# Attention scores from four 32-row slices of TensorE, and the softmax shift moved from GpSimd into ScalarE's exponentials

## The reference

```python
# both layers: 16 heads of depth 16, 77 context rows
logits = einsum('bhqd,bhkd->bhqk', q, k)      # layer 0: q scaled, + bias; layer 1: mask
weights = softmax(logits, axis=-1)            # over the 77 context rows
attn = einsum('bhqk,bhkd->bhqd', weights, v) @ Wo.T
# layer 0 experts: 32, the best four of each row
scores = softmax(flat @ router_w.T + router_bias)
topk_scores, topk_idx = top_k(scores, 4)
topk_scores = topk_scores / topk_scores.sum()
```

## Time and profile before

| | |
|---|---|
| runs of the kernel | 785.07 us median of 3 (783.95 to 786.47) |
| profiled execution | 784.07 us |
| its span, first to last instruction | 782.2 us |
| TensorE's mean granted clock | 0.981 of full |

### The profile page before, as it was taken

The page is one execution under the profiler, slowest core; times in us unless marked ns, Lnnn a source line. Parts: engine busy times, 40 slices in busy tenths (PEclk is TensorE's granted clock), DMA queues, the critical chain, the costliest instruction groups (busy, mean ns, idle before and its releaser), DMA issues.

```text
span 782.2 us, 15464 instructions
## 1 busy us (share of the span) xinstructions
PE 729.4 (93%) x4576; PEld 592.1 (76%) x4577; DVE 457.4 (58%) x1697; ACT 324.7 (42%) x1000; POOL 306.5 (39%) x331
## 2 busy tenths in 40 slices
PE   8799999999998999999999799988997999999994
PEld 4578888856665888888875488777774999999993
DVE  2689999647973544444433779999984232232331
ACT  1345555422221455555543488877850212212210
POOL 1243443300022555555514667763113244344421
PEclk9999999899999999999999999999998999999998
DMA  7423433340014455555872236776521565555530
GB/s 208 150 95 97 141 108 127 109 128 21 14 54 88 140 160 162 163 163 161 135 128 68 68 92 184 218 202 177 154 68 52 188 201 162 194 196 162 196 130 5
DMA packets 64181, 103.05 MB, mean 132 GB/s; under 512 B 20145, under 2 KB 42113, under 8 KB 63860
## 3 DMA queue, kind: packets, MB, share of 16 engines
q1 hardware_dynamic: 52852, 72.88, 29.9%
q0 software_dynamic: 10976, 27.22, 14.1%
q10 hardware_dynamic: 288, 2.10, 0.8%
HBM read 82.83 MB, written 22.07 MB: 134 GB/s over the span
## 4 chain that ended last, share of the span: by engine, by line
PE 64%; DVE 27%; DMA 3%; issue 2%; ACT 2%; POOL 1%; SPq 0%; DVEq 0%; ACTq 0%; POOLq 0%
PE bank L1368 11%; PE bank L1383 10%; PE bank L1316 9%; PE bank L937 5%; DVE U L1626 5%; PE bank L1329 5%; PE bank L1240 4%; DVE mx L1497 3%; DVE X L1488 2%; PE bank L844 2%; PE bank L1307 2%; PE bank L1288 2%; PE bank L923 2%; DMA expert_out<-U 2%; DVE R L1856 2%
## 5 line engine op out<-in xcount | busy, mean ns | idle before, releaser
L622 POOL DMA_INDIRECT U<-normed,idx_all x95 | 90.3, 951 | 141.8 <-PE bank L1307 73.7
L1316 PE MATMUL bank<-R,U 128*128 x380 | 99.2, 384 | 0.1
L1368 PE MATMUL bank<-X,R 128*128 128x128 f32 x736 | 85.9, 275 | 0.0
L1368 PEld LDWEIGHTS bank<-X,R 128*128 128x128 f32 x736 | 84.1, 192 | 0.1
L1383 PE MATMUL bank<-R,X 128*128 (+1 forms) x368 | 83.1, 379 | 0.0
L1977 DVE TENSOR_TENSOR U<-U,bank 128x128 f32<-128x128 f32 x95 | 27.3, 287 | 83.0 <-ACT U L804 82.9
L597 POOL DMA_INDIRECT R<-expert_out,slot x64 | 61.5, 960 | 35.1 <-DMA expert_out<-xr 17.7
L1383 PEld LDWEIGHTS bank<-R,X 128*128 128x128 f32 x368 | 68.2, 190 | 8.4
L691 ACT ACTIVATE U<-U,mx 128x77 f32<-128x77 f32 x256 | 67.3, 352 | 12.6 <-DVE mx L1497 12.6
L1316 PEld LDWEIGHTS bank<-R,U 128*128 128x128 f32 x380 | 65.4, 192 | 5.6 <-issue 0.3
L609 POOL TENSOR_TENSOR U<-U,mx 128x1232 f32<-128x1232 f32 x16 | 36.0, 2249 | 68.9 <-DVE mx L1497 68.9
(11 more groups left out here) (255 smaller groups left out, 1541.2 us busy)
## 6 DMA issues: line engine op xcount, KB each, us to landing
R<-in_w SPq DMA_DIRECT2D x21, 1024.0 KB
R<-in_w SPq DMA_DIRECT2D x40, 256.0 KB
R<-in_gu SPq DMA_DIRECT2D x8, 1024.0 KB, 5.8
expert_out<-U SPq DMA_DIRECT2D x48, 128.0 KB
expert_out<-xr SPq DMA_DIRECT2D x47, 128.0 KB
normed<-xr SPq DMA_DIRECT2D x32, 128.0 KB, 3.1
R<-in_down SPq DMA_DIRECT2D x8, 512.0 KB, 3.6
x<-X SPq DMA_DIRECT2D x16, 128.0 KB
```

The lines of the kernel that those rows point to most:

```text
L622: pool.indirect_dma_start(xg0[i % NXG], None, xn_d[0], bass.IndirectOffsetOnAxis(idx_all[:, i:i + 1], 0)).then_inc(EX[0]["gath"][i % NXG], 16)
L1316: mm = pe.matmul(bank[2 + u][:, 0:2 * F0], xgT0[u][:, c, :], gu_w[:, c, bass.ds(e, 1), :].rearrange("p a n -> p (a n)"), start=(c == 0), s ...
L1368: mm = pe.matmul(bank[1 + 2 * v + f // 4][:, (f % 4) * P:(f % 4 + 1) * P], w1_of[v][:, c, f * P:(f + 1) * P], xgT1[v][:, c, :], start=(c = ...
```

## The change

It does four things.

1. The rows of Wq and Wk (and their biases) are permuted on the host so that bank g's heads lie in rows 32g to 32g+31 of both chunks. `kbd` now holds 2 heads for 32 partitions, 32 rows by 154 columns, and `scores` issues eight matmuls, four row slices of chunk 0 and then four of chunk 1. Both releases of `sc_mm` come in chunk 1, after the sixth and the eighth matmul.
2. In attention 0 GpSimd's subtraction and ScalarE's single exponential go; VectorE negates its maxima there too, and ScalarE takes 16 exponentials per tile, heads 0 to 7 ahead of the third `pT` copy. At t=-1, where there is no `pT` yet, all 16 stand behind `qT`, in attention 1 as well.
3. `dve.max` writes to a tile's own slot of `best0`; the 16 subtractions of the best logit become one of 128x64, at the start of layer 0's experts.
4. In attention 0, `chosen0` of the tile before comes ahead of the cast of the indices.

```diff
+QH, QR = HG // KC, P // NG
-        kbd[0], o = cut(R2, o, (B * KC, HG, S2))
+        kbd[0], o = cut(R2, o, (B * KC, QH, S2))
...
-                    if l == 0 and on(t, 2):
-                        u = par(2)
-                        pool.wait_ge(T["mx"], 2 * n + 6)
-                        s3 = sc[u].rearrange("p (h k) -> p h k", h=H)
-                        pool.tensor_tensor(s3, s3, mx[u][:, :].unsqueeze(2).to_broadcast([P, H, S2]),
-                                           ALU.subtract).then_inc(T["sub"], 1)
...
-                    if l == 1 and on(t, 1):
+                    if on(t, 1) and on(t, 0):
                         ins = exps(t, n, 0)
...
-                    if l == 0 and on(t, 1):
-                        u = par(1)
-                        act.wait_ge(T["sub"], n + 2)
-                        act.activation(sc[u], sc[u], ACT.Exp).then_inc(T["p"], 1)
-                    if l == 1 and on(t, 1):
+                    if on(t, 1) and not on(t, 0):
+                        exps(t, n, 0)
+                    if on(t, 1):
                         exps(t, n, 1).then_inc(T["p"], 1)
...
-                    for g in range(NG):
-                        pe.wait_ge(T["q"], n + 3)
-                        if g % 2 == 0:
-                            need(pe, T["copied"], 2 * n + 3 + g // 2)
-                        c, half = g // 2, g % 2
-                        r = slice(64 * half, 64 * half + 64)
-                        mm = pe.matmul(bank[g][:, 0:HG * S2], qT[r, c, :],
-                                       kbd[l][r, batch(t, 2) * KC + c].rearrange("p h k -> p (h k)"),
-                                       start=True, stop=True)
-                        if half:
-                            mm.then_inc(T["sc_mm"], 1)
+                    pe.wait_ge(T["q"], n + 3)
+                    for c in range(KC):
+                        for g in range(NG):
+                            if c == 0 and g % 2 == 0:
+                                need(pe, T["copied"], 2 * n + 3 + g // 2)
+                            r = slice(QR * g, QR * g + QR)
+                            mm = pe.matmul(bank[g][:, c * QH * S2:(c + 1) * QH * S2], qT[r, c, :],
+                                           kbd[l][r, batch(t, 2) * KC + c].rearrange("p h k -> p (h k)"),
+                                           start=True, stop=True)
+                            if c == KC - 1 and g % 2:
+                                mm.then_inc(T["sc_mm"], 1)
...
-                                      ALU.max, negate=(l == 1)).then_inc(T["mx"], 1)
+                                      ALU.max, negate=True).then_inc(T["mx"], 1)
...
-                        dve.tensor_scalar(wgt[:, bass.ds((t - 2) * TOPK, TOPK)], m8[w][:, 0:TOPK], m8[w][:, 0:1],
-                                          None, ALU.subtract).then_inc(RT["below"], 1)
...
+                    dve.tensor_tensor(wgt[:, :].rearrange("p (t j) -> p t j", t=NT), best0[:, :, 0:TOPK],
+                                      best0[:, :, 0:1].to_broadcast([P, NT, TOPK]), ALU.subtract).then_inc(RT["below"], 1)
```

More of the change, by code:

```diff
@@ L58 @@
 NOH = NT
-TEMP_END = 9276
+TEMP_END = 8660
 VF_BACK = 632
@@ L136, in build @@
             attn_w[1][name], o = cut(U, o, (KC, D))
-        kbd[1], o = cut(U, o, (B * KC, HG, S2))
+        kbd[1], o = cut(U, o, (B * KC, QH, S2))
         vbd[1], o = cut(U, o, (B * PC, 3 * VC))
@@ L223, in build @@
         own_e, tile_less, tok_1 = route1[:, 0:E1], route1[:, E1:E1 + PLAN1], route1[:, E1 + PLAN1:]
-        mask_k = sb("mask_k", [P, HG])
+        mask_k = sb("mask_k", [P, QH])
         mask_v = sb("mask_v", [P, PC, 3])
@@ L247, in build @@
         m8 = [sb(f"m8_{i}", [P, 8]) for i in range(2)]
+        best0 = sb("best0", [P, NT, 8])
         i8 = [sb(f"i8_{i}", [P, 8], U32) for i in range(2)]
@@ L713, in step @@
                         transposed(n, 1)
-                    if l == 1 and on(t, 1):
+                    if on(t, 1) and on(t, 0):
                         ins = exps(t, n, 0)
-                        if t == NT - 2:
+                        if l == 1 and t == NT - 2:
                             ins.then_inc(T["p"], 1)
@@ L805, in _ @@
             experts0_steps(act, experts0)
-            act.wait_ge(RT["below"], NT)
+            act.wait_ge(RT["below"], 1)
             act.activation(wgt[:, :], wgt[:, :], ACT.Exp).then_inc(R0["exp"], 1)
@@ L1433, in keys @@
                         dve.tensor_tensor(kbd[l][:, b * KC + m],
-                                          k_sb[:, b * S2:(b + 1) * S2].unsqueeze(1).to_broadcast([P, HG, S2]),
-                                          mask_k[:, :].unsqueeze(2).to_broadcast([P, HG, S2]),
+                                          k_sb[:, b * S2:(b + 1) * S2].unsqueeze(1).to_broadcast([P, QH, S2]),
+                                          mask_k[:, :].unsqueeze(2).to_broadcast([P, QH, S2]),
                                           ALU.mult).then_inc(K["k_bd"], 1)
@@ L1513, in step @@
                     w, m = par(-2), n - 1
+                    best = best0[:, min(max(t - 2, 0), NT - 1), :] if l == 0 else m8[w][:, :]
                     if l == 0 and isinstance(t, int) and t == -2:
@@ L1542, in step @@
                         wait_apart(dve, RT["lg"], m)
-                        dve.max(m8[w][:, :], lg[:, 0:ne]).then_inc(RT["mx"], 1)
+                        dve.max(best, lg[:, 0:ne]).then_inc(RT["mx"], 1)
                     if l == 1 and on(t, -3):
@@ L1552, in step @@
                         wait_apart(dve, RT["mx"], m)
-                        dve.max_index(i8[w][:, :], m8[w][:, :], lg[:, 0:ne]).then_inc(RT["ix"], 1)
+                        dve.max_index(i8[w][:, :], best, lg[:, 0:ne]).then_inc(RT["ix"], 1)
                     if l == 1 and on(t, 3):
@@ L1562, in step @@
                         row_stats(T, par(3), t + 3)
-                    if l == 0 and on(t, -2):
-                        dve.tensor_scalar(wgt[:, bass.ds((t - 2) * TOPK, TOPK)], m8[w][:, 0:TOPK], m8[w][:, 0:1],
-                                          None, ALU.subtract).then_inc(RT["below"], 1)
                     if on(t, -1):
@@ L1576, in step @@
                                                  op1=ALU.add).then_inc(TL["slot"], 1)
+                    if l == 0 and on(t, -3):
+                        chosen0(t - 3)
                     if on(t, -2):
@@ L1579, in step @@
                         dve.tensor_copy(ef[:, bass.ds((t - 2) * nk, nk)], i8[w][:, 0:nk]).then_inc(RT["ef"], 1)
-                    if l == 0 and on(t, -3):
-                        chosen0(t - 3)
                     if l == 1 and on(t, -2):
@@ L1968, in experts0 @@
                 if isinstance(s, int) and s == 0:
+                    dve.wait_ge(RT["mx"], NT)
+                    dve.tensor_tensor(wgt[:, :].rearrange("p (t j) -> p t j", t=NT), best0[:, :, 0:TOPK],
+                                      best0[:, :, 0:1].to_broadcast([P, NT, TOPK]), ALU.subtract).then_inc(RT["below"], 1)
                     dve.wait_ge(bias_in[1], 16)
@@ L2026, in constants @@
         "ident": np.eye(P, dtype=np.float32),
-        "mask_k": ((p[:, None] % 64) // DH == np.arange(HG)).astype(np.float32),
+        "mask_k": ((p[:, None] % QR) // DH == np.arange(QH)).astype(np.float32),
         "mask_v": ((f // S2)[:, :, None] == (np.array(HEAD0)[None, :, None] + np.arange(3))).astype(np.float32)
@@ L2052 @@
     arrays["ctxT"] = rows_of(a["ctx_1024"].reshape(B * S2, D).T)
+    rows = np.arange(D).reshape(NG, KC, QH * DH).swapaxes(0, 1).reshape(D)
     for l in range(2):
         for w in ("Wq", "Wk", "Wv", "Wo"):
-            arrays[f"L{l}_{w}"] = rows_of(a[f"L{l}_xattn_{w}"].T)
+            m = a[f"L{l}_xattn_{w}"]
+            arrays[f"L{l}_{w}"] = rows_of((m[rows] if w in ("Wq", "Wk") else m).T)
     arrays["bias0"] = rows_of(a["fside_1x1xSxS2_0"].reshape(S, S2))
     arrays["mask1"] = rows_of(a["mask_BxSxS2_if1"].reshape(N, S2))
-    arrays["bqk"] = np.stack([a["L1_xattn_bq"].reshape(KC, P).T, a["L1_xattn_bk"].reshape(KC, P).T], 1)
+    arrays["bqk"] = np.stack([a["L1_xattn_bq"][rows].reshape(KC, P).T, a["L1_xattn_bk"][rows].reshape(KC, P).T], 1)
     arrays["bv"] = a["L1_xattn_bv"].reshape(1, D)
```

## The result

| | before | after |
|---|---|---|
| median | 785.46 us of 4 (783.95 to 786.47) | 795.90 us of 4 (792.32 to 799.18) |
| profiled execution, its span | 784.07, 782.2 | 797.71, 795.9 |
| mean granted clock | 0.981 | 0.954 |
| attention 0, first to last `rs` | 121.8 | 129.9 |
| attention 1, first to last `rs` | 126.4 | 137.8 |

The change makes the kernel 1.3% slower: ratio 1.0132, interval 1.0087 to 1.0176, or +10.4 us. The forecast was +6.1 us (791.2 from 785.07) with a chance of 0.60 for slower; the result lies inside the range and inside the main case's own range.

What follows compares the result with a forecast made beforehand. No single bound: a loop over three engines in attention 0, VectorE in steady attention 1. Terms -3.2, clock +7.8 and +1.5 gave +6.1 on 784.07, 790.2; the median runs 1.0 higher: 791.2 us, range 780.5 to 797.

Steps and rivals of the forecast that it cites:

- main case: The granted clock falls repeatedly, mostly in attention 1's steady steps: chance 0.60, own range 787.5 to 797 us.
- The clock, +9.3 forecast: Shorter scores and longer TensorE waits bring the clock down in steady steps: +7.8 us in attention 1, +1.5 in attention 0.
- six falls of 1.3 us: Attention 1's steady steps: 6 clock falls taken, bounds none and one in each of 12 steps, 1.3 us each, +7.8.
- one fall, +1.5: Attention 0: the same place is denser and TensorE has about 0.5 us of slack; one clock fall, +1.5 us.
- The sum without the clock, -3.2: Both heads, attention 0's steps, scores and keys together, before any clock falls in the steady steps: -3.2 us.
- Attention 1's head, -3.1: Attention 1's pipeline fill: `qT` ahead of the exponentials starts scores and transposes earlier; gain 3.1 us (1.5 to 3.6).
- Attention 0's head, -2.35: Attention 0's pipeline fill: exponentials without GpSimd's subtraction save 1.5 us, the clock staying up 0.85; gain 2.35 (1.2 to 2.8).
- Attention 0's steady steps, +0.28 each: Steps 2 to 13: eight exponentials delay the last `pT` copy, scores start 0.28 us later per step, +3.4 us (2 to 9).
- rival (b): ScalarE becomes attention 0's bound; at 0.7 us a step, 786.9 us without falls, 796 with them; chance 0.05 without falls.
- The last step but one, forecast at +0.3: Step 14 of attention 0: the same delay, less what the removed L1565 gives back, +0.3 us.
- The scores, 0.8 us for the block: Four 32-row slices side by side: about 0.8 us against 1.31; -0.9 us (0 to -1.5) in two steps of attention 1.
- Keys: Attention 1's keys, built between shared expert and experts: half the elements save 0.3 us a pair, two pairs, -0.6.

Runs made afterwards that it cites:

- run 3: The changed kernel plus three filler matmuls of 512 columns, result unread, behind the scores of each step from 0 on: 782.73 us, ratio 0.9962.
- run 5: The kernel before with only `qT` ahead of all sixteen exponentials in attention 1's step -1: 800.67 us on the second chip; repeated on the third, 780.65 us, ratio 0.9932.
- runs 1 and 6: The kernel before with 32-row scores and smaller keys alone, 796.8 us, ratio 1.0125; the same with each slice's two matmuls in turn, 812.22 us, ratio 1.0143.
- run 7: The kernel before, 64-row scores kept, plus two spare reciprocals ahead of `rs` in every step of attention 1: 784.79 us, ratio 0.9993.
- run 2: The changed kernel with scores, keys and weights put back to those of before (64-row pairs), all else changed: 783.79 us, ratio 0.9968.
- Run 4: The changed kernel with attention 0's first eight exponentials moved behind the last `pT` copies and the `qT` copy: 795.61 us, ratio 1.0110.

## Why the prediction was right

**The clock, +9.3 forecast.** Right in place and kind, too small in number. The changed kernel against run 3, where only the filler differs, is 1.0132 to 0.9962, 13 us. In attention 1 the forecast had six falls of 1.3 us. The trace has eight stretches at 1.2 GHz from first to last `rs`, which is 11.5 / 8 = 1.4 us for each. The price held. The number was a free choice between none and twelve, so that it came out only two low is luck. One stretch was longer, 513.7 to 524.0.

The reason given for the place was in part a misreading: not every steady step has TensorE waiting 1.15 us for `o_sb`. In the kernel before it stands in seven steps, from 507.30 to 562.03 (0.52 to 1.25 us), and in none ahead of them. The first fall of the changed kernel's steady part (493.19) comes in a step that had no such wait.

In attention 0 the forecast had one fall, +1.5; the profiled execution has three stretches at 1.2 GHz ahead of its last step and loses 5.8 us in four steps (9.88, 9.38, 9.47 and 10.65 us long, against 8.72 for the first and 8.30 for the others). Not all of that is the change's: run 5's kernel, with the old scores, loses as much in its first two steps (9.45 and 10.06 in its repeat). The two later ones, 3.5 us, may be: no profile with the old scores has one there. But neither have runs 1 and 6, with the new scores and the old softmax, so they seem to need both; that was not taken apart. Step 14 gives 1.5 back, since the clock is low for one stretch of 3.4 us there and not for the two of the earlier trace rows. That is not the change's either: run 7 and the repeat of run 5, with the old scores, have the one stretch too.

The rule of the Trainium skill, page "TensorE: Matmul & The Clock Gate", section "Why this matters for your kernels", that long idle gaps bring the clock down, does not cover these falls: TensorE was busy 2.89 of 3.42 us ahead of one, with no wait over 0.53.

**The sum without the clock, -3.2.** Run 3, which holds the clock up in attention 1, measured -3.0 (0.9962; -5.5 to -0.5). That this is so near to -3.2 is luck as well, since some terms below did not come as put and the interval is wide. By terms:

- Attention 1's head, -3.1: measured -3.4 between first scores and first `rs`, of which 0.5 comes back in the next two steps where these are undisturbed; by itself (run 5, repeated) -3.5 to -7.1 in the whole. Right.
- Attention 0's head, -2.35: of the two parts, 1.5 for the softmax and 0.85 for the clock, the first came, at 1.3. The second failed, and the step was "I take that the clock stays up for this stretch": in the changed kernel TensorE stood 5.14 us and the transposes took 1.11. Six profiles have the new softmax for tile 0; the clock fell in the head in five of them, among them run 3 after a wait of only 2.82 us, and stayed up in run 2. With the old softmax it stayed up once too (run 5's repeat). So the clock there is not the change's to give. In the changed kernel's own trace the 1.3 is taken by the maximum, 1.52 us later.
- Attention 0's steady steps, +0.28 each: exact, 8.30 us, by the copy named. But the sentence was only half of it: "what enters the loop is ScalarE's order". Run 4 shows that with the other order its work enters, at 8.28; rival (b)'s bound lies 0.02 us under the one forecast. The last step but one, forecast at +0.3, took 0.5 to 0.9 more (7.18 before; 7.70, 7.83 in run 3, 8.10 in run 2).
- The scores, 0.8 us for the block: 0.81. Their gain on the path, -0.9, was put too high. The 0.5 behind attention 1's head is not there: the head takes 14.6 us with either form (run 2 and the repeat of run 5 with 64-row scores, the changed kernel and run 3 with 32-row ones). Of the 0.4 before the end, 0.26 is (7.37 to 7.11 us), and with the filler nothing (7.47).
- Keys: a pair takes 0.55 instead of 0.87, and both pairs together 0.64 us less, as forecast. Whether that reaches the total is not shown. From the keys to attention 1's first scores the kernel before took 188.4 us, with the fall at 253.98. That fall is in no other profile, and without it this takes 185.2 to 187.8 us, with either size of keys. So most of the -2.7 between the attentions is not the change's.

By stage the forecast and the profiled pair differ more than the totals do: attention 0's head -2.35 against +0.2, its steps +5.2 against +8.1, between the attentions -0.6 against -2.7, attention 1's head -3.6 against -3.4, attention 1 after it +7.4 against +11.5. Errors of both signs met.

## What to carry to other kernels

Making a matmul block thinner or shorter can cost more clock than the block saves, as it did here: look for stretches just before a fall, and for stretches that resemble them without one, before taking work away. If the block is not on the path, filler matmuls in the time that it freed can pay; here they cost nothing and were worth 13 us on the first chip. And take the parts of a change apart: one reordered pair of steps in the pipeline's head, tried alone, reached as much as every version of the whole, as far as the intervals tell. And before a gain in a pipeline's head is put down to an edit, compare profiles at the same granted clock there.

## What the hardware showed that was not expected

- TensorE at 2.4 GHz fell to 1.2 after waits of 0.53 us, busy 2.89 of 3.42 us, when the scores used 32-row slices; with 64-row pairs it stayed up behind waits of 1.34. Not each such place costs the clock (0.54 us and busy 2.76 of 3.41 did not), and on the second chip it fell with 64-row pairs too, in steps of 9.7 to 13.8 us.
- Eight matmuls of 32 rows by 154 columns took 0.81 us slice by slice and 0.83 with each slice's two in a row: the order of the row slices did not matter.
- VectorE looked full in attention 1 (19.33 of 20 us), yet 0.36 us more a step moved the total by nothing that could be measured (0.9993), and its busy time in the same 20 us rose only to 19.61.
- The same kernel took 785.0, 785.45 and 800.9 us on three chips. The difference lay in the first steps of attention 1, in the kernels profiled there; of the kernel before there is one profile only, of an execution of 784.07 us.
